# Memory and expert block: four chunks of lookahead, an order of work written out by hand, and the sine products on GpSimd

## What is computed

```python
# L1_attn: a memory with rotating phases, over time within a sequence
dt      = softplus((x @ W_dt1 + b_dt1) @ W_dt2 + b_dt2)
phi     = cumsum(dt, axis=time) * omega_base
content = (x @ W_B + b_B) * x
c, s    = cumsum(content * cos(phi)), cumsum(content * sin(phi))
read    = c * cos(phi) + s * sin(phi)
y       = ((x @ W_C + b_C) * read) @ W_out + b_out + D * x

# L1_ffn: one shared expert and 4 of 16 small ones, chosen in 2 of 4 groups
scores  = softmax(x @ gate_w.T)                  # groups by maximum, then top 4
out     = shared(x) + sum over chosen e of score_e * (silu(x @ w1_e) * (x @ w3_e)) @ w2_e
```

## Time and profile before

| | us |
|---|---|
| median of 3 runs | 1529.39 (1526.48 to 1530.39) |
| the three runs | 1530.39, 1526.48, 1529.39 |
| the profiled execution: time from its first to its last instruction (span) | 1530.5 |
| TensorE busy | 1318.1 (86%) |
| VectorE busy | 1026.1 (67%) |
| ScalarE busy | 796.0 (52%) |
| GpSimd busy | 536.5 (35%) |
| the block of the change | 673.2 to 1038.9 of the span |

### The profile page before, as it was taken

One profiled execution on the slowest core, in us unless ns is written; L12 is line 12 of the kernel. 1 busy time (PEld: TensorE's weight loads), 2 busy tenths in 40 slices (PEclk: granted clock), 3 DMA queues, 4 the chain that ended last, 5 costly groups with the idle time before them and its releaser, 6 DMA issues. The chain is left out here.

```text
span 1530.5 us, 23116 instructions
## 1 busy us (share of the span) xinstructions
PE 1318.1 (86%) x7350; PEld 782.0 (51%) x7350; DVE 1026.1 (67%) x2781; ACT 796.0 (52%) x1595; POOL 536.5 (35%) x678
## 2 busy tenths in 40 slices
PE   5899999999997877953579999988899988989898
PEld 1223333333332677941335566557676756877633
DVE  7778888888882675645887786423567563666586
ACT  2467777777775203536546554322445452466554
POOL 3442443342210005439546434431112122443046
PEclk7799999999999888985689999999999999999999
DMA  5211111111101702210033323221132131100001
GB/s 152 61 33 42 54 48 34 50 51 43 43 23 50 185 1 55 64 39 24 14 91 72 62 57 56 57 56 40 60 102 75 60 115 56 35 1 1 1 21 35
DMA packets 80779, 81.23 MB, mean 53 GB/s; under 512 B 19899, under 2 KB 64139, under 8 KB 80659
## 3 DMA queue, kind: packets, MB, share of 16 engines
q1 hardware_dynamic: 77327, 74.06, 18.0%
q0 software_dynamic: 2304, 4.72, 1.4%
q10 hardware_dynamic: 1028, 0.98, 0.2%
HBM read 64.32 MB, written 13.92 MB: 51 GB/s over the span
## 5 line engine op out<-in xcount | busy, mean ns | idle before, releaser
L939 DVE TENSOR_REDUCE a_nm<-a_aps 128x1 f32<-128x512 f32 x512 | 333.7, 686 | 76.8 <-PE a_aps L704 76.7
L903 ACT ACTIVATE a_prob<-a_sps 128x512 f32<-128x512 f32 x512 | 271.5, 597 | 116.3 <-PE a_sps L716 115.3
L704 PE MATMUL a_aps<-a_K,a_Q 96*128 96x512 bf16 x512 | 195.9, 403 | 13.1 <-DMA a_K<-k_parts 12.7
L716 PE MATMUL a_sps<-a_Q,a_K 99*128 99x512 bf16 x512 | 156.9, 386 | 1.2 <-ACT a_prob L903 1.2
L1399 POOL TENSOR_TENSOR p_h<-p_sl,p_t 128x512 f32<-128x512 f32 x72 | 106.5, 1494 | 140.9 <-ACT p_sl L1542 86.5
L725 PE MATMUL a_ops<-a_prob,a_Vg 128*32 128x512 f32 x1024 | 137.2, 610 | 0.0
L704 PEld LDWEIGHTS a_aps<-a_K,a_Q 96*128 96x128 bf16 x512 | 50.4, 98 | 141.4 <-DVE a_nm L939 90.5
L1542 ACT ACTIVATE p_sl<-p_up_a 128x512 f32<-128x512 f32 x72 | 42.9, 597 | 109.1 <-PE p_up_b L1427 109.1
L413 POOL CAST a_ms<-a_mr 16x128 bf16<-16x128 f32 x32 | 9.0, 280 | 245.2 <-ACT a_mr L861 245.1
L1937 POOL TENSOR_TENSOR c_h<-c_h,c_G 128x512 f32<-128x512 f32 x24 | 34.1, 1427 | 171.7 <-DMA c_G<-choice_rows 112.9
L716 PEld LDWEIGHTS a_sps<-a_Q,a_K 99*128 99x128 bf16 x512 | 50.1, 99 | 61.5 <-ACT a_prob L903 30.5
(11 more groups left out here) (585 smaller groups left out, 2794.2 us busy)
## 6 DMA issues: line engine op xcount, KB each, us to landing
p_G<-gates_by_expert SPq DMA_DIRECT2D x32, 512.0 KB, 10.6
c_G<-choice_rows SPq DMA_DIRECT2D x32, 512.0 KB, 6.5
a_Q<-q_parts SPq DMA_DIRECT2D x192, 32.0 KB
a_K<-k_parts SPq DMA_DIRECT2D x31, 96.0 KB
q_parts<-a_partsq SPq DMA_DIRECT2D x7, 384.0 KB, 2.8
k_parts<-a_partsk SPq DMA_DIRECT2D x7, 384.0 KB, 2.8
token_outputs<-m0e_y SPq DMA_DIRECT2D x40, 64.0 KB, 1.5
m0w_w<-in_L_ffn_W SPq DMA_DIRECT2D x1, 2048.0 KB, 8.9
```

The source lines that it names most:

```text
L704: nc.tensor.matmul(aps[n % 3][:, :], Q[0:MAX, head, q * P:(q + 1) * P], K[0:MAX, head, :], start=True, stop=True).then_inc(a_ready, 1)
L716: nc.tensor.matmul(sps[(NS * u + k) % 3][:, :], K[0:KB, head, k % TC * P:(k % TC + 1) * P], Q[0:KB, head, :], start=True, stop=True).then_ ...
L903: nc.scalar.activation(prob[u % 2][:, k // TC, k % TC, :], sps[n % 3][:, :], ACT.Exp).then_inc(p_done, 1)
L939: nc.vector.tensor_reduce(nm[u % 2][:, s:s + 1], aps[n % 3][:, :], AX.X, ALU.max, negate=True).then_inc(a_used, 1)
```

## The change

In words, with the lines of the new code where they differ:

- The loop of one pattern is replaced by an opening and a step 0 that are written out for each engine, and a loop for steps 1 to 7.
- Less lies ahead: in step s the memory of chunk s+2 (was s+3), the first transpose, time steps and input gates of s+3 (was s+5 and s+4), the fetch's addition of s+4 (was s+8). The fetched rows lie in a ring of five buffers.
- VectorE normalises chunks 0 and 1 first, and chunk 0 a second time.
- Chunk 0's gates don't go through DRAM: for each pair TensorE multiplies a table of zeros and ones (`of_pair`) with the turned gates and ScalarE copies the result (`choose_pair`, `keep_pair`).
- On VectorE the phase is cut in two (`phase_sum` between the steps, `phase_rest` behind product 0) and so is the choice (`choose_groups` between the steps, `choose_experts` behind product 1).
- For chunks 1 to 7 (`BY_POOL`) GpSimd makes the two products with the sine, behind its third and sixth h of a step; VectorE waits for them in `sum_sines` and `read_memory`.
- In the middle of a step TensorE runs `outer` first, and `down` goes expert by expert, each waiting for its own h, with the second transpose behind the second and the logits behind the fourth.

```diff
+    NB = 5
...
+            def turn_content(c):
+                pool.wait_ge(content_made, BY_POOL.index(c) + 1)
+                nc.gpsimd.tensor_tensor(cs[:, :], content[:, :], sn[c % 2][:, :], ALU.mult).then_inc(cs_made, 1)
+
+            def turn_memory(c):
+                pool.wait_ge(mem_made, BY_POOL.index(c) + 1)
+                nc.gpsimd.tensor_tensor(cs[:, :], mem[:, :], sn[c % 2][:, :], ALU.mult).then_inc(ms_made, 1)
...
+            fetch_back(0)
             nc.gpsimd.memset(one[:, :], 1.0)
             nc.gpsimd.memset(half_pi[:, :], math.pi / 2).then_inc(consts, 1)
+            fetch_back(1)
+            nc.gpsimd.tensor_scalar(Dg[:, :], net.ident[:, :], Dc[:, :], None, ALU.mult).then_inc(diag, 1)
             nc.gpsimd.memset(gs[:, :, GROUPS:], -1.0)
             nc.gpsimd.memset(cur[:, :, E:], -1.0).then_inc(padded, 1)
-            nc.gpsimd.tensor_scalar(Dg[:, :], net.ident[:, :], Dc[:, :], None, ALU.mult).then_inc(diag, 1)
-            fetch_back(0)
-            for s in steps:
+            fetch_back(2)
+            add_bias(0)
+            nc.gpsimd.memset(of_pair[:, :, :], 1.0).then_inc(pair_ones, 1)
+            pool.wait_ge(pair_ones, 1)
+            nc.gpsimd.affine_select(out=of_pair[:, :, :], in_=of_pair[:, :, :], compare_op=ALU.is_ge, fill=0.0,
+                                    base=0, pattern=[[P, NP], [1, P]], channel_multiplier=-I).then_inc(pair_low, 1)
+            pool.wait_ge(pair_low, 1)
+            nc.gpsimd.affine_select(out=of_pair[:, :, :], in_=of_pair[:, :, :], compare_op=ALU.is_ge, fill=0.0,
+                                    base=I - 1, pattern=[[-P, NP], [-1, P]], channel_multiplier=I).then_inc(pairs_made, 1)
+            add_bias(1)
+            first_normal(2)
+            add_bias(2)
+            fetch_back(3)
+            fetch_back(4)
+            for s in range(B):
                 for j in range(NW):
-                    if here(s):
-                        inner_units(s, j)
-                if here(s + 6):
-                    first_normal(s + 6)
-                if 1 <= s + 9 < B:
-                    fetch_back(s + 9)
+                    inner_units(s, j)
+                    if s == 0 and j == 0:
+                        turn_content(1)
+                        turn_memory(1)
+                    if s == 0 and j == 5:
+                        first_normal(3)
+                        add_bias(3)
+                    if s == 0 and j == 6:
+                        turn_content(2)
+                        turn_memory(2)
+                    if s > 0 and here(s + 2) and j == 2:
+                        turn_content(s + 2)
+                    if s > 0 and here(s + 2) and j == 5:
+                        turn_memory(s + 2)
+                if here(s + 4):
+                    first_normal(s + 4)
+                    add_bias(s + 4)
+                if here(s + 5):
+                    fetch_back(s + 5)
...
+                    pe.wait_ge(xT2_done, 1 if c == 0 else min(c + 2, B))
+                    pe.wait_ge(z_read, min(c + 3, B))
+                if u == 1:
+                    pe.wait_ge(shifted, 1)
...
-            def down(c, k):
-                if k == 0:
-                    pe.wait_ge(h_done, NW * (c + 1))
+            def down(c, j):
+                if j == 0:
                     wait(pe, y_added, c)
-                for j in range(NW):
+                pe.wait_ge(h_done, NW * c + j + 1)
+                for k in range(TC):
                     last = nc.tensor.matmul(yps[:, k, :], h[c % 2][:, j, k * P:(k + 1) * P], w2[:, expert(j), :],
-                                            start=(j == 0), stop=(j == NW - 1))
-                if k == TC - 1:
+                                            start=(j == 0 and k == 0), stop=(j == NW - 1), skip_group_check=True)
+                if j == NW - 1:
                     last.then_inc(y_done, 1)
...
+            def choose_pair(j):
+                if j == 0:
+                    pe.wait_ge(gT_done, 1)
+                    pe.wait_ge(pairs_made, 1)
+                wait(pe, G0_done, j)
+                nc.tensor.matmul(whole_yps, of_pair[:, j, :], gT[0][:, :], start=True, stop=True).then_inc(chosen, 1)
...
+            def middle(s):
+                pe.wait_ge(a_done, NW * (s + 1))
+                if here(s + 2):
+                    outer(s + 2)
+                if here(s + 3):
+                    turn_first(s + 3)
+                pe.wait_ge(t_done, NW * (s + 1))
+                if here(s + 3):
+                    steps_of_time(s + 3)
+                    input_gates(s + 3)
+                for j in range(NW):
+                    down(s, j)
+                    if j == 1 and here(s + 2):
+                        turn_second(s + 2, up_a[1])
+                    if j == 3 and here(s + 2):
+                        logits(s + 2, up_b[1])
...
+            for s in range(1, B):
                 for j in range(NW):
-                    if here(s):
-                        up(s, j)
...
-                if s >= 0 and here(s + 3):
-                    outer(s + 3)
...
-                if here(s):
-                    for k in range(TC):
-                        down(s, k)
+                    up(s, j)
...
+            def keep_pair(j):
+                act.wait_ge(chosen, j + 1)
+                nc.scalar.activation(G[0][:, j, :], whole_yps, ACT.Copy).then_inc(G0_done, 1)
...
+            def sum_sines(c):
+                if c in BY_POOL:
+                    v.wait_ge(cs_made, BY_POOL.index(c) + 1)
+                last = nc.vector.tensor_tensor_scan(mem[:, :], one[:, :], cs[:, :], 0.0, ALU.mult, ALU.add)
+                if c in BY_POOL:
+                    last.then_inc(mem_made, 1)
+                v.drain()
...
+            def read_memory(c):
+                if c in BY_POOL:
+                    v.wait_ge(ms_made, BY_POOL.index(c) + 1)
+                tt(cc[:, :], cc[:, :], cs[:, :], ALU.add)
+                v.drain()
+                wait(v, o_done, c - 1)
+                stt(r[c % 2][:, :], cps[:, :], bC[:, :], cc[:, :], ALU.add, ALU.mult).then_inc(r_done, 1)
...
+            def middle(s):
+                if here(s + 4):
+                    add_back(s + 4)
+                if here(s + 2):
+                    add_memory(s + 2)
+                    second_rstd(s + 2)
+                if here(s + 4):
+                    first_rstd(s + 4)
+                if here(s - 1):
+                    measure_output(s - 1)
+                if here(s + 2):
+                    shift_logits(s + 2, up_b[1])
+                    choose_groups(s + 2)
+                if here(s + 3):
+                    phase_sum(s + 3)
...
+            product(0, 0)
+            take_content(1)
+            turn_content(1)
+            sum_cosines(1)
+            sum_sines(1)
+            product(0, 1)
+            turn_back(1)
+            product(0, 2)
+            read_memory(1)
+            product(0, 3)
+            add_back(3)
+            add_memory(1)
+            phase_sum(2)
+            second_rstd(1)
+            first_rstd(3)
+            product(0, 4)
+            phase_rest(2)
+            product(0, 5)
+            shift_logits(1, ops)
+            product(0, 6)
+            take_content(2)
+            turn_content(2)
+            sum_cosines(2)
+            sum_sines(2)
+            choose_groups(1)
+            choose_experts(1)
+            product(0, 7)
+            turn_back(2)
+            product(0, 8)
+            read_memory(2)
+            middle(0)
...
+            for s in range(1, B):
+                    product(s, j)
+                    if j == 0 and here(s + 2):
+                        phase_rest(s + 2)
+                    if j == 1:
+                        if here(s + 1):
+                            choose_experts(s + 1)
+                    if here(s + 2):
+                        if j == 2:
+                            take_content(s + 2)
+                        if j == 3:
+                            turn_content(s + 2)
+                        if j == 4:
+                            sum_cosines(s + 2)
+                        if j == 5:
+                            sum_sines(s + 2)
+                        if j == 6:
+                            turn_back(s + 2)
+                        if j == 7:
+                            read_memory(s + 2)
+                middle(s)
+            add_output(B - 1)
+            measure_output(B - 1)
```

More of the change, by code:

```diff
@@ L1641, in _ @@
+            keep_gates(1, ops)
+            middle(0)
+            for s in range(1, B):
+                for j in range(NW):
+                    silu(s, j)
+                    if here(s + 2) and j == 2:
+                        trig(s + 2)
+                    if here(s + 1) and j == MID:
+                        keep_gates(s + 1, ops)
+                middle(s)
         @block.vector
```

364 lines of the change are left out of this document (211 added, 153 removed).

## The result

The changed kernel takes 1553.49 us (median of 4 runs, 1552.68 to 1557.59), the kernel before 1528.37 (4 runs): a ratio of 1.0163, 95% interval 1.0145 to 1.0181. That is slower, as forecast, and within the range of 1519 to 1557, but +25 where the forecast said +13, and outside the forecast's own 1533 to 1550. The profiled execution of the changed kernel is its slowest run (1557.59, span 1555.9), 4 us above its median.

The account below looks back on a forecast made before the run. TensorE was taken to bound steps 1 to 5, a chain through all five engines the opening. Opening -12, full steps +29, steps 6 and 7 -4 gave +13: 1529.4 to 1542 us, range 1519 to 1557.

Parts of the forecast that it names:

- Opening and step 0: From the block's start to step 1: step 1 begins at 805 instead of 817.0, 12 us won, bounds 795 and 812.
- The walk's stations: Moments in opening and step 0: memory(0) ends 713.1, first up 727, r(1) 746.5, r(2) 787, step 1 at 805.
- r in a full step: On VectorE in steps 1 to 5: r ready 24.5 us after the step's start, 3.6 of it waits.
- the two places: VectorE behind products 0 and 1, where phase_rest and choose_experts stand: each costs a wait for GpSimd of up to 1.2 us.
- The third wait: VectorE's read_memory, for GpSimd's second multiplication at the end of the chain to r: some 1.2 us.
- From r to the next step: TensorE's output product, time steps, input gates and down products behind r: 14.3 us, making a full step 38.8.
- Rival B: Second normalisation 1.5 us late, idle TensorE falls to 1.2 GHz, some 2 us a step: steps of 41, 1554; chance 0.18.
- B's own sign: What would show the slower-clock rival: a granted clock well below 0.9 in steps 1 to 5.
- Rival A: VectorE comes first at SBUF and GpSimd waits: steps of 35.2, in all -4.4 to -6, 1524; chance 0.22.
- Rival C: The opening gives more: step 1 at 795, full steps as forecast, +3 in all, 1532; chance 0.15.
- A's threshold: A full step of 36.1 us, below which the change is faster than the kernel before.
- Steps 6 and 7: Last steps with the tail: down products start as each h comes, 4 us won of 57.5.

Follow-up runs that it names:

- x2_pieces_middle: Changed kernel with the phase's reduction and the choice's second half back between ups and down, GpSimd's multiplications kept: 1540.54 us, ratio 1.0077 to the kernel before.
- x5_filled: Changed kernel with three unread matmuls of 512 columns added in each of steps 0 to 5 before the output product: 1544.02 us, ratio 1.0088 to the kernel before.
- x8_phase_early_vector: Changed kernel with both phase halves behind the memory's addition, time step before output product, all sine products on VectorE: 1527.96 us, ratio 1.0002 to the kernel before.
- x1_vector_sine: Changed kernel with all multiplications by the sine back on VectorE: 1556.58 us, ratio 1.0182 to the kernel before.
- x11_copy_first: x10_choice_earlier with the first copy of chunk s+3 ahead of the exponential's table load on ScalarE: 1516.05 us, ratio 0.9912 to the kernel before.
- x4_downs_first: Changed kernel with the transpose of chunk s+3 and four down products ahead of the output product on TensorE: 1540.71 us, ratio 1.0061 to the kernel before.
- x10_choice_earlier: x9_output_early with the second half of the choice behind product 0 instead of product 1: 1527.65 us, ratio 0.9939 to the kernel before.
- x9_output_early: Changed kernel with phase behind the memory's addition, output product directly behind the time step, second copy and maximum's subtraction moved: 1530.01 us, ratio 0.9956 to the kernel before.

## Why the prediction was right in sign and short in size

*Opening and step 0: right, in part by luck.* Forecast -12 with step 1 at 805; it came at 802.57, -15.3 from the barrier on. The walk's stations: first up 727 (726.0), r(1) 746.5 (745.4), sines of chunk 2 at 773 (771.2), r(2) 787 (785.8). The last stretch, r(2) to step 1, took 16.7 instead of 18. One station is off: memory(0) ended at 715.5, not 713.1, and from there to the first up it took 10.4 instead of some 14, so that two errors nearly cancel.

*r in a full step: right.* Forecast 24.5 after the step's start, with 3.6 for waits; it is 23.95, 24.15, 23.8 and 23.8. x2_pieces_middle confirms the price of the two places (0.90 and 1.11 against 1.2 each). The third wait has the right size and another form: GpSimd's second multiplication was late by only 0.33, and the addition that follows it was drawn out by 1.05.

*From r to the next step: the term that was mis-sized.* The forecast added 14.3; it is 16.84 (884.37 less 867.53). Down products, input gates and logits have the lengths given. Two things are missing. `outer` was put at 1.8 as in the earlier trace rows, where TensorE comes to it busy; behind 3.4 us of idle time it takes 3.4, which x5_filled undoes. And between `turn_first` and the time step stands a copy on ScalarE, which before was covered by other products: 1.34 from L1515 to L1530 instead of 0.5. That makes 2.5 a step; r was 0.35 earlier than forecast; so 40.8 instead of 38.8, and 38 instead of 29 over five steps. That the opening won 3 us more than forecast covers a third of these 9.

*Rival B* named the first of these and gave it 2 us a step. Its other half, a cover too short for the second normalisation, is not there: no wait stands ahead of L1522 in the rows of step 2 (in step 5 there is one of 2.38). B's own sign, a granted clock well below 0.9 in steps 1 to 5, did not appear: it was 0.91 to 0.96. The time is B's 1554, the reason is half B's, and 5 us of the time are in no rival at all.

*Rival A fell:* the operations were drawn out as forecast. *Rival C* was met in part: the opening gave more, 3 us and not 10. A's threshold is near the mark: the change was to be faster below a full step of 36.1, and the kernels at 35.3, 35.8 and 36.6 are, by 0.9, 0.6 and 0.5%, while x8_phase_early_vector at 37.2 equals the kernel before and x2_pieces_middle at 39 is slower.

*Steps 6 and 7:* -4 forecast, -3.5 measured.

*What was not in the sum:* the 5.1 us behind the block. The same instructions take 491.5 in before, 496.6 and 495.2 in the two profiles of the changed kernel, and in x1_vector_sine, whose instructions behind the block are the same too:

```profile
1065.93:1554.30 488.37, 436.45 (x2559) 314.50 (x2559) 300.60 (x929) 248.27 (x535) 140.72 (x147) 0.99 0.15 47
```

x5_filled has 488.4, x11_copy_first 486.7. TensorE's busy time goes with it, from 436 to 444 for 2559 matmuls, and the granted clock from 0.99 to 0.97. With 495.2 in its second profile on another chip, the changed kernel's is hardly chance in one execution; x4_downs_first and x10_choice_earlier have 495.4 and 494.5 too. That the moment at which the later stages meet their idle times decides it is my reading; no run here shows it, and it stays open.

*What stays of "the change":* its opening is worth 15 us and its shorter lookahead costs what the full steps lose, since output product, second normalisation, logits and choice of one chunk all lie in one step. The order of before keeps them in different steps and has full steps of 30 to 36.6 us. The parts of the loop that were to blame could be moved, and with full steps of 36.6 and less the sum turns.

## What to carry to other kernels

When a reorganisation shortens the lookahead, look for the loop it closes: follow one item from its last consumer back to the same engine's next turn, and price that loop with every in-order neighbour in it, not the engines' busy times. Price a product that will stand behind idle time at either clock: the output product behind 3.4 us ran at the lower one, and behind 1.9 us it went either way (x10_choice_earlier and x11_copy_first). And when a wait is removed, look one engine further for what was just as late: here VectorE, then TensorE's order, then ScalarE's table loads bound the same step. And read an edit from the stretch that it changes, not from the total alone.

## What the runs showed of the hardware

- An operation on 128 by 64 elements, 0.23 us by itself, takes 1.34 beside GpSimd's products; VectorE's products, which read one operand from PSUM, keep their 0.65 to 0.69 in every kernel. In x9_output_early even a multiplication by a constant (L1829, one input in SBUF, 0.42 in the changed kernel) took 1.15 where it met GpSimd's addition of the output bias. The Trainium skill, SBUF — State Buffer, section "Who interferes with whom", says that such an operation can be shut out as well if it runs in a two-port mode; the 1.15 fits that, but no trace here shows the mode.
- 2.8 us of extra matmuls that nobody reads made each full step 1.1 to 1.6 us shorter, and full steps at a granted clock of 1.00 had 31.4 us of TensorE work where the changed kernel's, at 0.96, had 33.3.
- Stages in which nothing is changed differ by up to 10 us between kernels (486.7 to 496.6), 0.6% of the whole time. A difference of that size between two kernels isn't proof that the changed part did it; the changed part's own length is.
